# Every second projection-weight load on GpSimd's queue, and the LayerNorm gain applied by VectorE instead of ScalarE

## The reference

```python
# x: [8, 4096, 1024]
x = x + retention(layernorm(x))       # q,k,v = h @ W_qkv, rotary, decay mask, group norm,
                                      # gate = silu(h @ W_g), (gate * normed) @ W_proj
x = x + ffn(layernorm(x))             # z = layernorm * ln_g + ln_b
                                      # z_sent = mean(z) over tokens -> router picks one expert
                                      # y = relu(z @ W_down[e] + b) @ W_up[e] + b, times gate
```

## Time and profile before

| | us |
|---|---|
| median of 2 runs | 3282.46 (3262.91 to 3302.01) |
| profiled execution, time | 3283.62 |
| its span, slowest core (core 6) | 3282.0 |
| spans of the 8 cores | 3243.3 to 3282.0 |
| busy: TensorE / VectorE / ScalarE / GpSimd | 1703.1 / 1188.2 / 712.0 / 207.1 |

### The profile page before, as it was taken

The page is one execution under the profiler, slowest core; times in us unless marked ns, Lnnn a source line. Parts: engine busy times, 40 slices in busy tenths (PEclk is TensorE's granted clock), DMA queues, the critical chain, the costliest instruction groups (busy, mean ns, idle before and its releaser), DMA issues.

```text
span 3282.0 us, 28992 instructions; the slowest of 8 cores (3243.3 to 3282.0 us)
## 1 busy us (share of the span) xinstructions
PE 1703.1 (52%) x8110; PEld 855.2 (26%) x8174; DVE 1188.2 (36%) x2165; ACT 712.0 (22%) x1324; POOL 207.1 (6%) x336
## 2 busy tenths in 40 slices
PE   0066555555646556555646465565555555653133
PEld 0022322323232323223222323232222223232121
DVE  1013335252515143352525251524435252515334
ACT  0012223121222213221222222222223121221100
POOL 0100000000000000000000000000000000000100
PEclk7576777686866777666768677777777686866555
DMA  7883343544352433434353534344243444332466
GB/s 130 107 207 109 107 157 101 167 135 167 128 173 91 148 140 109 155 96 167 128 173 129 173 114 162 103 134 167 95 158 107 167 133 143 128 122 66 141 236 224
DMA packets 156947, 459.25 MB, mean 140 GB/s; under 512 B 14197, under 2 KB 26486, under 8 KB 146294
## 3 DMA queue, kind: packets, MB, share of 16 engines
q1 hardware_dynamic: 110262, 277.02, 26.3%
q0 software_dynamic: 37312, 113.26, 12.7%
q10 hardware_dynamic: 9216, 67.11, 5.3%
HBM read 432.17 MB, written 58.72 MB: 150 GB/s over the span
## 4 chain that ended last, share of the span: by engine, by line
PE 35%; DVE 20%; ACT 16%; DMA 15%; issue 10%; POOL 2%; DVEq 1%; ACTq 1%; POOLq 0%; SPq 0%
DMA wp<-wproj_bf 6%; PE PA L572 6%; DMA wqkvg_bf<-wqkvg 4%; PE PA L506 4%; PE PB L506 3%; PE PA L759 3%; PE PC L382 3%; PE PB L759 3%; PE PC L572 3%; PE PD L572 3%; ACT v_sb L582 2%; DMA outT<-out_sb 2%; DVE gst L697 2%; DVE gst L694 2%; POOL xp_sb L773 2%
## 5 line engine op out<-in xcount | busy, mean ns | idle before, releaser
L572 PE MATMUL PA<-wnb,lnx_sb 128*128 128x512 bf16 x1007 | 343.8, 426 | 49.3 <-ACT v_sb L582 27.7
L572 PE MATMUL PC<-wnb,lnx_sb 128*128 128x512 bf16 x497 | 210.2, 423 | 231.0 <-ACT v_sb L582 205.4
L759 PE MATMUL PA<-ggT_sb,wp 128*128 128x256 bf16 x1024 | 244.5, 329 | 135.6 <-DMA wp<-wproj_bf 108.0
L371 DVE TENSOR_TENSOR ao_sb<-qs_sb 128x1024 bf16<-128x1024 bf16 x64 | 44.3, 692 | 649.3 <-ACT qs_sb L368 649.3
L506 PE MATMUL PA<-wnb,lnx_sb 128*128 128x512 bf16 x496 | 171.4, 427 | 170.2 <-DMA wnb<-wqkvg_bf 152.1
L759 PE MATMUL PB<-ggT_sb,wp 128*128 128x256 bf16 x1024 | 244.1, 328 | 23.8 <-ACT pe_sc L770 23.8
L572 PE MATMUL PD<-wnb,lnx_sb 128*128 128x512 bf16 x511 | 217.3, 425 | 17.4 <-ACT v_sb L582 6.0
L382 PE MATMUL PC<-qs_sb,ones_bf 128*1 128x256 bf16 x256 | 59.7, 413 | 240.9 <-ACT qs_sb L368 240.9
L506 PE MATMUL PB<-wnb,lnx_sb 128*128 128x512 bf16 x497 | 170.4, 426 | 4.0 <-ACT qbf L517 2.5
L453 POOL DMA_DIRECT2D wnb<-wqkvg_bf x128 | 69.5, 543 | 1488.4 <-PE PB L506 1018.0
L759 PEld LDWEIGHTS PA<-ggT_sb,wp 128*128 128x128 bf16 x1024 | 109.0, 116 | 201.7 <-issue 174.6
(11 more groups left out here) (216 smaller groups left out, 2740.7 us busy)
## 6 DMA issues: line engine op xcount, KB each, us to landing
wnb<-wqkvg_bf SPq DMA_DIRECT2D x256, 512.0 KB, 5.9
wp<-wproj_bf SPq DMA_DIRECT2D x256, 512.0 KB, 6.0
wnb<-wqkvg_bf POOLq DMA_DIRECT2D x128, 512.0 KB, 4.9
x<-xt ACTq DMA_DIRECT2D x16, 1024.0 KB, 4.9
tab<-tabs ACTq DMA_DIRECT2D x16, 1024.0 KB, 7.0
xp<-xp_sb ACTq DMA_DIRECT2D x16, 1024.0 KB, 7.9
x<-xp POOLq DMA_DIRECT2D x16, 1024.0 KB, 8.0
outT<-out_sb ACTq DMA_DIRECT2D x16, 1024.0 KB, 4.3
```

Source lines behind the costliest of these rows:

```text
L371: S.op("vector", lambda E, a=a, b=b: E.tensor_tensor(xsq_fl[:, a:b], xbf_fl[:, a:b], xbf_fl[:, a:b], ALU.mult), reads=[xbf_fl[:, a:b]], wr ...
L572: S.op("tensor", lambda E, m=m, k=k, P=P, wb=wb: E.matmul(P, lnx_sb[:, k, m * 128:(m + 1) * 128], wb[:, k % 4, :], start=(k == 0), stop=(k ...
L759: S.op("tensor", lambda E, vtp=vtp, sub=sub, vt=vt, f=f, P=P, fo=fo: E.matmul(P[:, fo:fo + C], wp_sb[vtp % 4][:, sub, f * 128:(f + 1) * 12 ...
```

## The change

Two edits. In `load_wp` the steps with odd `vtp` are issued by GpSimd's queue instead of SP's; even ones stay on SP. In `b1_rest` the 8 multiplications by the gain are done by VectorE (`tensor_scalar`) instead of ScalarE (`activation` with a scale). Buffers, sizes and program order are as before.

```diff
     def load_wp(vtp):
         iv_ = d_wproj_bf[vtp * 256:(vtp + 1) * 256, :].rearrange(
             "(two p) n -> p two n", p=128)
-        S.dma("sync", lambda E, o=wp_sb[vtp % 4], i=iv_: E.dma_start(out=o[:], in_=i),
+        S.dma("sync" if vtp % 2 == 0 else "gpsimd",
+              lambda E, o=wp_sb[vtp % 4], i=iv_: E.dma_start(out=o[:], in_=i),
               reads=[d_wproj_bf[vtp * 256:(vtp + 1) * 256, :]], writes=[wp_sb[vtp % 4][:]])
@@ b1_rest
         for k in range(KF):
-            S.op("scalar", lambda E, k=k: E.activation(
-                out_sb[:, k, :], out_sb[:, k, :], AF.Copy, scale=lng[:, k:k + 1]),
+            S.op("vector", lambda E, k=k: E.tensor_scalar(
+                out_sb[:, k, :], out_sb[:, k, :], lng[:, k:k + 1], None, ALU.mult),
                 reads=[out_sb[:, k, :], lng[:, k:k + 1]], writes=[out_sb[:, k, :]])
```

## The result

The changed kernel is slower: a median of 3346.16 us against 3278.69, ratio 1.0217 with a 95% interval of 1.0182 to 1.0252. That is clear of no change; whether it is more or less than 2% the interval leaves open. The prediction said no change that can be measured (3293 us, 3240 to 3335), so the measured time lies above its range. Of the two edits one did what was forecast and a little more, the other cost nearly twice its price.

The account below looks back on a forecast made before the run. The prediction took no engine as the bound, but a chain of hand-overs. From 3283.6 us it took 87.9 for the gain on VectorE and added 97 for wave 1's loads, giving 3293 us, range 3240 to 3335.

Parts of the forecast that it names:

- The 6.1 us at L382: TensorE's wait at L382 in 13 rounds: it starts 6.1 us earlier with the gain on VectorE, 79.8 us in all.
- The eight operations: Gain multiplications on VectorE: 8 x 0.53 = 4.2 us, all covered by waiting for ScalarE's cast.
- The sum of 88 us: Gain of edit two over all rounds: 79.8 + 6.8 + 1.3 = 87.9 us saved.
- Loads 1 and 3 of wave 1: On GpSimd behind its adds: load 1 issued at E + 3.9 (E: wave 0's end), step 1 starts at E + 8.9.
- Load 7: Wave 1, GpSimd: issued 14.1 us after wave 0, meets SP's eight `wnb` loads, takes 7.0, lands at 21.1.
- Step 7 at half clock: Wave 1: slow 1.70 us steps charged to steps 1 to 3; after load 7 at 21.1 the wave ends at 22.1.
- the sum had 97: Cost of wave 1's loads: 6.2 us a round in 15 rounds, 4.1 in the last, +97 us.
- Wave 0: Its odd loads on GpSimd: nothing gained or lost, DMA engines being full; taken as 0.
- The high end of 202 us: Upper bound for edit one: 8.0 us for each GpSimd load, 12.6 us a round in 16 rounds.
- that side: Rival that loads on GpSimd are dear, 8.0 us each: 3398 us, chance 0.11.
- the 8.0 us case: Each `wp` load on GpSimd takes 8.0 us, the price of a 1024 KB load there: 3398 us, chance 0.11.
- the number of pieces: Mechanism of the dear-loads rival: GpSimd's price goes with pieces, `wp` rows being 2 KB, not 4 KB; chance 0.11.

Follow-up runs that it names:

- w1_13_sp: Changed kernel with loads 1 and 3 of wave 1 back on SP: 3235.68 us, ratio 0.9920 to the kernel before.
- adds_dve: Changed kernel with the adds into xp_sb on VectorE instead of GpSimd: 3206.56 us, ratio 0.9818 to the kernel before.
- w0_again: Changed kernel with all wave 1 loads on SP, only odd loads of wave 0 on GpSimd, second run: ratio 0.9757 to the kernel before.
- gain_again: Kernel before with only the gain multiplications moved to VectorE, all projection loads on SP, run again: ratio 0.9679 to the kernel before.
- after_4kb: Changed kernel with W_proj's bf16 copy laid out as one 4 KB piece per partition and load: 3355.09 us, ratio 1.0266 to the kernel before.
- gain_half: Kernel before with gain on VectorE, each wave loading only its half of W_proj's columns, 256 KB a step into 8 buffers: 3070.85 us, ratio 0.9377.
- gain_half_dve: gain_half with the adds into xp_sb on VectorE: 3013.47 us, ratio 0.9213 to the kernel before.

## Why the prediction was wrong

- **Edit two** was right step by step. The 6.1 us at L382 were 6.2. The eight operations took 3.57 us rather than 4.2, all hidden. The sum of 88 us was measured at 96 and 105. Each round is 7 us shorter outside the projection: 6.2 at L382, 0.15 more between there and wave 0, and 0.6 before ScalarE's last drain, a stretch that the edit was not expected to touch; why is not shown.
- **Loads 1 and 3 of wave 1**: right in mechanism and size. Step 1 was forecast at 8.9 and started at 9.3, load 1 taking 5.3 us and not 4.9; the 0.4 was made up again by step 4 (13.9, forecast 14.0). w1_13_sp and adds_dve show that it was the place behind the adds.
- **Load 7 is the term that failed.** Step 3 ends at 13.9, as forecast at 14.0, and then GpSimd takes half a microsecond to issue the load, at 14.7 where 14.1 was forecast. The prediction saw the crowd and gave it 7.0 us, "nearer the crowd" between 4.9 and the 7.5 of the earlier trace rows. It took 8.6 in the mean, so step 7 starts at 23.4 and not 21.1. The load of that row had two loads of SP issued within 0.7 us ahead of it and three behind; load 7 meets load 6 and three weight loads ahead and five behind. Choosing a value below that row was the wrong direction.
- **Step 7 at half clock.** TensorE had then idled for over 5 us, and its last step took 1.7 and not 1.05 (1.3 in the mean in the kernel before); the mean granted clock of that step fell from 0.83 to 0.59. The windows view of the changed kernel, in the columns of the earlier trace rows, with the granted clock at 0.50 (1.2 GHz) around that step:

```profile
1524.00:1529.00 5.00, 1.44 (x7) 1.02 (x8) 0.00 (x0) 0.00 (x0) 0.00 (x0) 0.50 1.02 335
```

  The prediction had charged the slow clock to the steps after the first wait, but not to the one after the second. The issue 0.6 late, the landing 1.6 longer and this step 0.65 longer, with 0.15 from landing to start, make the 3.0 by which wave 1 ends later than forecast (25.1, not 22.1). Wave 1 thus cost 147 us where the sum had 97. The change cost 71 us where the sum had 9, which is 62 short: 50 are here and 10 to 20 in wave 0; the gain gave some 10 more than forecast, which goes the other way, and the 9 us behind the last projection remain.
- **Wave 0** was taken as free because the DMA engines were full either way. That reason holds for how much is moved, not for how soon a load is issued. In the changed kernel wave 0 costs 10 us on average and 19 on the four slowest cores; in w0_again against gain_again 18 and 28.
- **The rivals and the range.** The high end of 202 us for the loads was in the text, and the measured 174 lay within it, but only 0.11 was given to that side and the range ended at 3335, below even the 8.0 us case. The error was in tying that end to a mechanism that looked unlikely (the number of pieces, refuted by after_4kb) instead of asking how wrong the crowd term could be for any reason. 2 us more on load 7 alone already make 30.

## What to carry to other kernels

Before a DMA is put on another engine's queue, list what stands ahead of it there (here four adds that wait for the end of the wave) and what it no longer stands ahead of in the old one (here 4 MB of prefetch for later). Each cost some 60 to 100 us here, while no run shows a gain from the second issuer. When a term rests on a contended row, take its value from a case at least as crowded, and add the slow clock after every new wait, not only the first. And ask of a stream that is bound by loads whether it loads things that it doesn't use.

## What the runs showed of the hardware

- A load of 512 KB on GpSimd's queue took 8.6 us beside SP's stream of eight, 4.8 without it.
- With the odd loads of wave 0 on GpSimd's queue, one core of each neighbouring pair took 239 us for its 16 waves 0 and the other 219 (w0_again); with all on SP all eight took 208 to 216 (gain_again).
- After 5.77 us without a matmul TensorE's granted clock was 0.50 in the next step of 8 matmuls, which took 1.7 us. Step 1 of wave 1 took 1.51 us at a mean of 0.62 in gain_half and 0.87 us at 1.00 in gain_half_dve, where it starts 1.2 us sooner after wave 0.
- GpSimd issued a load 0.54 us after TensorE released it, SP 0.08 us. Its issue took 722 ns for 256 pieces of 2 KB and 537 ns for 128 of 4 KB; SP's took 359 and 320.
- VectorE's `tensor_scalar` on f32 128x256 in SBUF with a gain per partition, eight in a row, each waiting for the last, took 3.57 us: 0.46 from start to start and not 0.53.
